# A four-layer network on one core: each attention head stacked in 48 rows, two heads side by side in TensorE's rows, four slots for keys and queries, dummy matmuls in the ramp, two small products on GpSimd

## What is computed

```python
q, k, v = split(x @ W_q.T), split(x @ W_k.T), split(x @ W_v.T)
attn = softmax(scale * einsum('bnqd,bnkd->bnqk', q, k), axis=-1)
o = einsum('bnqk,bnkd->bnqd', attn, v)
```

## Time and profile before

| | |
|---|---|
| median of three runs | 748.71 us (748.31 to 750.13) |
| the profiled execution | 747.71 us, span 745.9 us |
| TensorE matmuls busy | 642.7 us (86%) |
| VectorE busy | 433.6 us (58%) |
| ScalarE busy | 392.8 us (53%) |
| GpSimd busy | 59.1 us (8%) |
| mean granted clock | 0.929 |

### The profile page before, as it was taken

One profiled execution on the slowest core, in us unless ns is written; L12 is line 12 of the kernel. 1 busy time (PEld: TensorE's weight loads), 2 busy tenths in 40 slices (PEclk: granted clock), 3 DMA queues, 4 the chain that ended last, 5 costly groups with the idle time before them and its releaser, 6 DMA issues.

```text
span 745.9 us, 9973 instructions
## 1 busy us (share of the span) xinstructions
PE 642.7 (86%) x3441; PEld 427.8 (57%) x3441; DVE 433.6 (58%) x860; ACT 392.8 (53%) x748; POOL 59.1 (8%) x89
## 2 busy tenths in 40 slices
PE   2755698799989989799989988799899988999896
PEld 0411477354468767544477777444478776543585
DVE  0451595688274655877364756886365737883344
ACT  1432477156864564257764564267755572368710
POOL 2010320300000002100000003000000004000000
PEclk9856799689999999899999999799999999699999
DMA  8997430521000005220000005220000013220000
GB/s 282 378 379 237 113 112 29 106 39 29 1 1 1 1 29 106 51 44 3 1 1 4 1 29 106 51 44 2 0 1 1 1 32 75 51 44 1 1 1 29
DMA packets 34483, 45.12 MB, mean 60 GB/s; under 512 B 4736, under 2 KB 27392, under 8 KB 34304
## 3 DMA queue, kind: packets, MB, share of 16 engines
q1 hardware_dynamic: 29728, 31.32, 15.0%
q0 software_dynamic: 3488, 10.49, 4.9%
q10 hardware_dynamic: 1216, 2.66, 1.4%
HBM read 28.45 MB, written 3.15 MB: 42 GB/s over the span
## 4 chain that ended last, share of the span: by engine, by line
PE 61%; DMA 11%; DVE 11%; ACT 10%; issue 4%; SPq 2%; ACTq 1%; DVEq 0%
PE psum L1215 28%; PE psum L1375 10%; PE psum L1437 7%; PE psum L1448 7%; DMA arena<-in_hyp_w 4%; DMA early_pieces<-in_hyp_w 3%; DVE mx L1032 3%; DMA kst<-split 2%; ACT arena L537 2%; PE psum L1476 1%; ACT kst L537 1%; ACT act L537 1%; PE psum L1303 1%; PE psum L1234 1%; PE psum L1337 1%
## 5 line engine op out<-in xcount | busy, mean ns | idle before, releaser
L714 ACT ACTIVATE arena<-psum 128x512 f32<-128x512 f32 x256 | 141.6, 600 | 89.6 <-PE psum L1437 88.5
L1032 DVE TENSOR_REDUCE mx<-psum 128x1 f32<-128x512 f32 x256 | 162.5, 683 | 41.9 <-PE psum L1375 41.6
L1375 PE MATMUL psum<-kst,qst 96*128 96x512 f32 x192 | 88.2, 511 | 20.7 <-DMA kst<-split 10.3
L1215 PE MATMUL psum<-act,ghw_hi 128*128 128x512 f32 (+1 forms) x288 | 89.6, 377 | 3.0 <-DVE act L833 2.5
L1437 PE MATMUL psum<-qst,kst 98*128 98x512 f32 x192 | 82.6, 452 | 1.9 <-ACT arena L714 1.3
L1375 PEld LDWEIGHTS psum<-kst,qst 96*128 96x128 f32 x192 | 43.0, 227 | 60.0 <-DVE mx L1032 35.6
L1215 PE MATMUL psum<-upw_hi,kst 128*128 128x512 f32 x256 | 71.3, 400 | 2.0 <-issue 1.5
L1448 PE MATMUL psum<-arena,vals 128*17 128x512 f32 x512 | 69.2, 613 | 1.3 <-ACT arena L714 1.0
L1215 PEld LDWEIGHTS psum<-act,ghw_hi 128*128 128x128 f32 x288 | 52.5, 190 | 15.3 <-DVE act L833 4.7
L434 POOL DMA_DIRECT2D kst<-split x36 | 17.7, 497 | 489.6 <-DMA kst<-split 407.6
L1215 PEld LDWEIGHTS psum<-upw_hi,kst 128*128 128x128 f32 x256 | 46.5, 189 | 11.7 <-issue 2.4
(11 more groups left out here) (184 smaller groups left out, 1079.9 us busy)
## 6 DMA issues: line engine op xcount, KB each, us to landing
early_pieces<-in_hyp_w SPq DMA_DIRECT2D x17, 512.0 KB, 9.3
arena<-in_hyp_w SPq DMA_DIRECT2D x15, 512.0 KB, 9.3
...
kst<-split POOLq DMA_DIRECT2D x36, 128.0 KB, 3.5
...
```

Of the source, the lines that this page charges most:

```text
L714: s.activation(probs[:, kb % 2, i, :], bank[3 + n % RING], ACT.Exp).then_inc(a_p, 1)
L1032: v.reduce_max(mx[:, g % 2, col:col + 1], bank[u % RING], AX.X).then_inc(d_max, 1)
L1215: ins = pe.matmul(dst, lhs(a, c), rhs(z, c), start=start and n == 0, stop=stop and n == len(terms) - 1, skip_group_check=skip)
L1375: pe.matmul(bank[u % RING], qst[g % 3][0:KROWS, i, P * t:P * t + P], keys_of(g)[0:KROWS, i // 2, :], start=True, stop=True).then_inc(e_max, 1)
```

## The change

KROWS becomes 48: the three parts of one head, 16 rows each, stand one under another, and the tile needs no zeros. Heads 0 and 2 of a group begin at row 0, heads 1 and 3 at row 64 (HALF_ROWS), two heads of a parity side by side in the free dimension. A maxima tile uses 48 rows, a score tile 50. `max_order` lets maxima tiles alternate between the halves, odd head first. Keys and queries have four slots each, one for each group; the fourth query slot is part of `act_both`. The moves are of 16 rows each, six for keys and six for queries of a group; the first group's keys are moved by ScalarE (two) and GpSimd (four). The rows of maxima are moved for even heads by SyncE (and once by ScalarE), for odd heads by GpSimd (`odd_rows`). The ones below the keys are written once, before the first batch, and no zeros are written. Dummies (`keep_clock`) stand in the ramp. The additions of `kept_output` and the products with alpha move to GpSimd.

```diff
 MAGIC = 12582912.0
 HYP_SCALE = 0.1
-KROWS = 3 * 32
+HALF_ROWS = 64
+KROWS = 3 * DH
 SROWS = KROWS + 2
...
-        kst = [sb(f"kst{i}", [P, G // 2, L], F32R) for i in range(3)]
         with nc.sbuf_tensor("early_pieces", [P, 2 * G * L], F32) as early_pieces:
             pass
-        qst = [sb(f"qst{i}", [P, G, L], F32R) for i in range(2)] + [act_both]
-        inp = kst[0:2]
+        kst = [sb(f"kst{g}", [P, G // 2, L], F32R) for g in range(NG)]
+        qst = [sb(f"qst{g}", [P, G // 2, L], F32R) for g in range(NG - 1)] + [act_both[:, 0:G // 2, :]]
+        inp = qst[1:3]
...
+        def rows_of(tile, i, rows):
+
+            at = HALF_ROWS * (i % 2)
+            return tile[at:at + rows, i // 2, :]
+
+        def stacked(tile, e, k):
+            at = HALF_ROWS * e + DH * k
+            return tile[at:at + DH, :, :].bitcast(F32)
+
+        def rows_in_split(g, e, part, first):
+            at = 32 * g + DH * e
+            return split[at:at + DH, 4 * part + first:4 * part + first + 2, :].bitcast(F32)
+
+        def maxima_row(g, k, e):
+            at = HALF_ROWS * e + KROWS + k
+            return qst[g][at:at + 1, :, :].rearrange("p i (t n) -> p (i t) n", t=T).bitcast(F32)
+
+        def maxima_of(k, e):
+            return mrow[k][2 * T * e:2 * T * e + 2 * T, :].bitcast(F32)
+
+        def max_order(r):
+
+            return 2 * (r // (2 * T)) + 1 - r % 2, r // 2 % T
...
             def stack_q(b, g):
 
-
-
                 if g == 0:
-                    sp.wait_ge(queries_zero, 2)
-                if g >= 3:
-                    sp.wait_ge(e_score, b * (NG * T * G) + T * G * (g - 2))
-                if g == 2:
-                    sp.wait_ge(act_zero, b + 1)
-                for e in range(2):
-                    for k, part in enumerate((0, 1, 0)):
-                        src = split[32 * g + DH * e:32 * g + DH * e + DH, 4 * part:4 * part + 2, :]
-                        dst = qst[g % 3][32 * k + DH * e:32 * k + DH * e + DH, e::2, :]
-                        sp.dma_start(dst.bitcast(F32), src.bitcast(F32)).then_inc(queries_in[e][g % 3], 16)
+                    sp.wait_ge(a_qk, b * 4 + 2)
+                if g == 1:
+                    sp.wait_ge(a_qk, b * 4 + 4)
+                    sp.wait_ge(d_qk, b * 4 + 4)
+                if g == 3:
+                    sp.wait_ge(e_maxT, b * NG + 1)
+                for k, part in ((0, 0), (2, 0), (1, 1)):
+                    if g == 0 and part == 1:
+                        sp.wait_ge(d_qk, b * 4 + 2)
+                    for e in range(2):
+                        sp.dma_start(stacked(qst[g], e, k), rows_in_split(g, e, part, 0)).then_inc(queries_in[g], 16)
...
-                for k, ready in enumerate((a_mrow, d_mrow)):
-                    if g == 0 and k == 0:
-                        continue
-                    sp.wait_ge(ready, b * NG + g + 1)
-                    sp.dma_start(maxima_row(g, k), mrow[k][:, :].bitcast(F32)).then_inc(rows_in, 16)
-
-            def results(first_done, rows):
+                if g >= 1:
+                    sp.wait_ge(a_mrow, b * NG + g + 1)
+                    sp.dma_start(maxima_row(g, 0, 0), maxima_of(0, 0)).then_inc(rows_in, 16)
+                sp.wait_ge(d_mrow, b * NG + g + 1)
+                sp.dma_start(maxima_row(g, 1, 0), maxima_of(1, 0)).then_inc(rows_in, 16)
...
-                for g in range(2):
+                for g in range(3):
                     stack_q(b, g)
                 maxima_rows(b, 0)
-                stack_q(b, 2)
+                stack_q(b, 3)
...
-            def stack_k(b, g):
-
-                if g >= 3:
-                    pool.wait_ge(keys_ones, b * 2 + 2)
-                    pool.wait_ge(e_score, b * (NG * T * G) + T * G * (g - 2))
-                    pool.sem_inc(keys_free, 1)
-                for k, part in enumerate((0, 0, 1)):
-                    src = split[32 * g:32 * g + 32, 4 * part + 2:4 * part + 4, :]
-                    pool.dma_start(keys_of(g)[32 * k:32 * k + 32, :, :].bitcast(F32), src.bitcast(F32)
-                                   ).then_inc(keys_in[g % 3], 16)
+            def stack_k(b, g, chunks=((0, 0), (1, 0), (2, 1))):
+
+                for k, part in chunks:
+                    for e in range(2):
+                        pool.dma_start(stacked(kst[g], e, k), rows_in_split(g, e, part, 2)).then_inc(keys_in[g], 16)
+
+            def odd_rows(b, g):
+
+                pool.wait_ge(a_mrow, b * NG + g + 1)
+                pool.sem_inc(keys_free, 1)
+                pool.dma_start(maxima_row(g, 0, 1), maxima_of(0, 1)).then_inc(odd_rows_in, 16)
+                pool.wait_ge(d_mrow, b * NG + g + 1)
+                pool.sem_inc(keys_free, 1)
+                pool.dma_start(maxima_row(g, 1, 1), maxima_of(1, 1)).then_inc(odd_rows_in, 16)
...
+            def kept_x4(b, h):
+
+                pool.wait_ge(d_kept_ff, b * 2 - 1 + h)
+                pool.sem_inc(keys_free, 1)
+                pair = slice(2 * h, 2 * h + 2)
+                pool.tensor_tensor(x4_tok[:, pair, :], kept_z[:, pair, :], x4_tok[:, pair, :], ALU.add
+                                   ).then_inc(p_kept_x4, 1)
...
             def batch(b, first=False):
-                pool.wait_ge(keys_hi_in, b * (2 * 16) + 2 * 16)
-                pool.wait_ge(keys_lo_in, b * 16 + 16)
+                pool.wait_ge(a_qk, b * 4 + 4)
                 pool.sem_inc(keys_free, 1)
+                stack_k(b, 0, ((1, 0),))
+                pool.wait_ge(d_qk, b * 4 + 4)
+                pool.sem_inc(keys_free, 1)
+                stack_k(b, 0, ((2, 1),))
                 stack_k(b, 1)
                 if not first:
                     kept_low(b, 0)
                 stack_k(b, 2)
                 if not first:
                     kept_low(b, 1)
-                    pool.wait_ge(p_kept_lo, b * 2)
-                    pool.sem_inc(keys_free, 1)
-                for i in range(2):
-                    pool.memset(kst[i][KROWS:SROWS, :, :].bitcast(F32), 1.0).then_inc(keys_ones, 1)
-                pool.wait_ge(keys_ones, b * 2 + 2)
-                pool.wait_ge(e_maxT, b * NG + 1)
-                pool.sem_inc(keys_free, 1)
-                pool.memset(qst[2][:, :, :].bitcast(F32), 0.0).then_inc(act_zero, 1)
-                pool.wait_ge(act_zero, b + 1)
                 stack_k(b, 3)
+                odd_rows(b, 0)
+                if not first:
+                    for h in range(2):
+                        kept_x4(b, h)
+                odd_rows(b, 1)
+                alphas(b, first)
+                for g in range(2, NG):
+                    odd_rows(b, g)
...
-                def first_keys(parts, ready, signal):
-
-                    s.wait_ge(ready, b * 4 + 4)
-                    for k, part in parts:
-                        src = split[0:32, 4 * part + 2:4 * part + 4, :]
-                        s.dma_start(keys_of(0)[32 * k:32 * k + 32, :, :].bitcast(F32), src.bitcast(F32)
-                                    ).then_inc(signal, 16)
-
-                first_keys(((0, 0), (1, 0)), a_qk, keys_hi_in)
+                s.wait_ge(a_qk, b * 4 + 4)
+                if first:
+                    s.wait_ge(keys_ones, NG)
+                for e in range(2):
+                    s.dma_start(stacked(kst[0], e, 0), rows_in_split(0, e, 0, 2)).then_inc(keys_hi_in, 16)
                 for h in range(2):
-                    if h == 1:
-                        first_keys(((2, 1),), d_qk, keys_lo_in)
...
                 v.tensor_tensor(kept_z[:, pair, :], bank[KEPT_ACC[h]].rearrange("p (t d) -> p t d", t=2),
                                 alpha[:, D:2 * D].unsqueeze(1).to_broadcast([P, 2, D]), ALU.mult
                                 ).then_inc(d_kept_ff, 1)
-                v.wait_ge(d_kept_ff, b * 2 + h - 1)
-                v.tensor_tensor(x4_tok[:, pair, :], kept_z[:, pair, :], x4_tok[:, pair, :], ALU.add
-                                ).then_inc(d_outs, 1)
...
                     v.tensor_copy(alpha[:, :], bank[7]).then_inc(d_alpha, 1)
-                    v.wait_ge(d_alpha, b + 1)
-                    v.tensor_tensor(alpha_ob[:, :], alpha[:, D:2 * D], outb[:, :], ALU.mult)
-                    if first:
-                        v.wait_ge(vow_in, 16)
-                    v.tensor_tensor(wo_alpha[:, :, :], vow[:, :, D:2 * D],
-                                    alpha[:, 0:D].unsqueeze(1).to_broadcast([P, C, D]), ALU.mult
-                                    ).then_inc(d_woalpha, 1)
...
-                    g, k, t = u // (G * T), u % (G * T) // T, u % T
-                    i = HEAD_ORDER[k]
-                    in_turn = 2 if g % 3 == 0 else 1
-                    if t == 0 and k % 2 == 0:
-                        pe.wait_ge(queries_in[k // 2][g % 3], b * (3 * 16 * in_turn) + 3 * 16 * (g // 3 + 1))
-                    if t == 0 and k == 0:
+                    g, (i, t) = u // (G * T), max_order(u % (G * T))
+                    if u % (G * T) == 0:
```

(33 more changed lines are left out.)

65 lines of the change are left out of this document (36 added, 29 removed).

## The result

The changed kernel takes 769.81 us (median of 4 runs, 764.67 to 774.45) where the kernel before took 749.42 on the same chip: a ratio of 1.027 (95% interval 1.022 to 1.033). It is slower by 20 us; 731.6 was forecast. The profiled execution took 769.22, with a span of 767.4.

The account below looks back on a forecast made before the run. TensorE was taken to set the pace of the attention rounds with maxima. Terms of -5.3 us in each of batches 1 to 3 and -1.2 in batch 0 gave -17.1, hence 731.6 us; forecast 726 to 737, wider range 720 to 744.

Parts of the forecast that it names:

- Packed tiles: First to ninth weighing: tiles in different array halves run at once, -4.5 us in batches 1 to 3, -3.5 in batch 0.
- the middle that I took: 24.3 us for the eight rounds, between a lower end of 21.9 and an upper end of 26.9.
- Mode switches: Layout changes at 0.1 us each: +0.6 us in the ramp of batches 1 to 3, +0.8 after the ninth weighing.
- Batch 0's dummies: A dummy behind each of batch 0's maxima tiles: 0.66 us a tile against 0.595, +0.8 us.
- its clock: Batch 0's maxima tiles: the half clock from 147.0 to 156.5 goes, -0.8 us.
- Dummies of batches 1 to 3: Ramp of batches 1 to 3: dummies hold the clock for the kept products, -1.3 + 0.5 = -0.8 us each.
- the clock still falls in the ramp: Rival: VectorE still paces the ramp and packed tiles leave TensorE more idle; about 742 us, chance 0.15.
- Kept additions: End of kept products to first weighing, batches 1 to 3: two additions leave VectorE; with these tiles' clock -2.4 us.
- alpha products: Products moved to GpSimd take 0.43 + 0.68 us off VectorE, already counted in the packed tiles' term.
- Rows of maxima: Odd heads' rows through GpSimd's queue land in 2.4 us; two of four groups stall a little, +0.6 us per batch.
- late moves: Rival: GpSimd's moves land late and delay each group's first score, 16 times; about 757 us, chance 0.09.
- Start of the ramp: First maxima tile waits for four GpSimd and six query moves, with more issues: +0.4 us per batch.

Follow-up runs that it names:

- e2: The changed kernel with batch 0's 21 + 4 dummies on 48 rows, in the array half of the tile ahead: 749.53 us, ratio 1.001.
- e6: e5 with all dummies of the change added, everything but the stacking in 48 rows: 728.88 us, ratio 0.974 to the kernel before.
- e1: The changed kernel without the dummy behind each maxima tile of batch 0 and the four behind them: 751.71 us, ratio 1.003.
- e5: The kernel before with only the kept additions and alpha products moved to GpSimd: 736.43 us, ratio 0.983.
- e3: The kernel before (96-row tiles) with the 14 + 21 + 4 dummies of 128 rows in batch 0: 748.35 us, ratio 0.999.
- e9: e6 with each of its new dummies on 48 rows instead of 128: 758.13 us, ratio 1.012 to the kernel before.
- e8: e2 with the second group's moves held until the first group's have landed: 744.91 us, ratio 0.993 to the kernel before.

## Why the prediction was wrong

The forecast of -17 became +20. Of these 37 us, 15.8 are batch 0's (forecast -1.2, measured +14.6) and 21.4 those of the other three (forecast -5.3 each, measured +2.0, +2.6 and +0.9). Two steps failed most: the price of batch 0's dummies, and the assumption that dummies hold the clock beside the stacked tiles. In batch 1 the start is 1.4 us longer than before, the first tile to the first score 5.4; the first score to the first weighing is 3.2 shorter and the eight rounds 2.5; the rest is 0.8 longer. By the prediction's own steps:

*Packed tiles, -4.5 and -3.5.* Right that tiles of different halves run at once; wrong in what it is worth. The eight rounds took 26.3 us, not 24.3. Where the clock was mostly held they took 24.5 (e2, batch 3):
```profile
651.50:676.00 24.50, 22.60 (x138) 7.74 (x136) 21.55 (x38) 17.42 (x35) 4.04 (x6) 0.94 0.01 2
```
Batch 0 of e2 took 24.6 at 0.95. So the middle that I took fits TensorE at nearly full clock, and the missing 1.8 us go with the clock. That it fits was luck: no row chose a point between 21.9 and 26.9 (whose middle is 24.4; the 26.4 in the prediction's last line is a slip). And of the 2.5 us that remain, 1.8 come without stacking: e6 has 27.0. The stacking gave 0.7 us for each batch here; with the clock mostly held it would be 2.5.

*Mode switches, +0.6 and +0.8.* The price of 0.1 us was taken from starts at an alpha matmul and a weighing. The rows shown now give 0.20 on the way into a 128-row matmul, 0.11 more behind it and 0.10 on the way back; only the last was priced right. In the ramp of batch 1 of e2, at full clock, 16 new switches cost 13.97 - 12.25 = 1.7 us net of the pairs, not 0.6. In the last group it was 1.2, of which 0.6 stays when the order is the same.

*Batch 0's dummies, +0.8, and its clock, -0.8.* This is the step that failed most. I priced tile, dummy and two switches at 0.66 us; they took 0.85, and at half clock 1.45. (Even by the 0.66 the sum is off: 21 tiles at 0.66 less 0.595 are 1.4 us, not 0.8.) Over VectorE's 0.6 each further tenth is paid 21 times, and the slower clock, which the dummies were to prevent and did not (0.63 and 0.50), raises the price again. Together 18 us (e1).

*Dummies of batches 1 to 3, -0.8.* "That they hold the clock is my assumption", it said, and the support was the clock of 1.00 in rounds of 96- and 98-row tiles. The assumption holds for those tiles: e6 against e5 gives 3.1, 1.4 and 2.4 us. It does not hold beside tiles of 48 rows: with the same dummies the ramp and the rounds of batch 1 have 0.89, 0.58, 0.76 and 0.85 where e6 has 1.00. That the rows matter is shown by e2 against e3; e9 against e6 agrees. The rival "the clock still falls in the ramp" was the right mechanism, but sized at 10 us from the kernel before's clock; that the stacking itself would lower the clock below what it had been, beyond the ramp too, was in none of the cases.

*Kept additions, -2.4, and alpha products.* Larger than forecast: e5 wins 13 us. First score to first weighing fell, in batch 1, from 8.55 us to 6.09 in e5 and 5.36 in the kernel after.

*Rows of maxima, +0.6.* A small GpSimd move lands in 1.6 us, not 2.4, and no first score of a group waits for one: the second and third groups' stretches are the shortest of all. The rival on the slower side, late moves, did not happen; the kernel ended beyond its time for another reason.

*Start of the ramp, +0.4.* It was 1.4 to 1.6 us in batches 1 to 3 and 0.9 in batch 0; a third to two thirds of it in batches 1 to 3, and a quarter in batch 0, went when the second group's moves were held back (e8).

What the stacking costs against e6 adds up: 16.9 us in batch 0 and 7.5, 8.1 and 7.8 in the others, 40.3 in all, the difference of the spans. In batch 1 that is start 1.3, ramp 3.2 (1.7 by e2 at full clock, which I put down to the switches, the rest clock), until the first score 3.2, first group 0.5, last group 1.2, less 1.8 in the two groups between.
